# A Hyena block and an adapter on one core: the order of the last stage's products on TensorE, and the rounds in which its steps stand

## What is computed

```python
def _hyena_fwd(x, ...):                       # x is layernorm(x)
    proj = (x @ in_proj_w + in_proj_b).reshape(B, L, C, ORDER + 1)
    v = short_conv(proj[..., 0]) + short_b
    coefs = (gelu(gelu(pos @ fw1 + fb1) @ fw2 + fb2) @ fw3 + fb3).reshape(L, C, ORDER)
    v_fft = rfft(v, n=2 * L, axis=1)
    for i in range(ORDER):
        conv = irfft(v_fft * rfft(coefs[:, :, i], n=2 * L, axis=0)[None], n=2 * L, axis=1)[:, :L, :]
        output = x_branches[i] * conv         # only the last i counts
    return output @ out_w + out_b
x = x + _hyena_fwd(layernorm(x), ...)
x = x + einsum('k,kod,bsd->bso', weights, W[ids], layernorm(x)) + einsum('k,ko->o', weights, b[ids])
```

## Time and profile before

| what | value |
|---|---|
| median of 3 runs (lowest, highest) | 2643.75 us (2641.79, 2646.72) |
| the profiled execution | 2646.0 us, its span 2644.2 us |
| busy over the span: PE, DVE, POOL, ACT | 2415.0, 1463.2, 969.1, 850.0 us |
| granted clock of PE, mean over the span | 0.978 |
| data moved by DMA | 496.59 MB, mean 188 GB/s |

### The profile page before, as it was taken

One profiled execution on the slowest core, in us unless ns is written; L12 is line 12 of the kernel. 1 busy time (PEld: TensorE's weight loads), 2 busy tenths in 40 slices (PEclk: granted clock), 3 DMA queues, 4 the chain that ended last, 5 costly groups with the idle time before them and its releaser, 6 DMA issues. The chain is left out here.

```text
span 2644.2 us, 39549 instructions
## 1 busy us (share of the span) xinstructions
PE 2415.0 (91%) x12804; PEld 1564.5 (59%) x12804; DVE 1463.2 (55%) x2188; ACT 850.0 (32%) x1151; POOL 969.1 (37%) x1189
## 2 busy tenths in 40 slices
PE   6689999999999999699999779989999999999998
PEld 2267777777777776243343356666666666666665
DVE  6634434444443433477776556666666666666665
ACT  3333443343343343244444312222222222222221
POOL 2322222222222222000000056666666666666664
PEclk9789999999999999799999889999999999999999
DMA  5543554544454453899999866555555555555553
GB/s 183 200 124 128 193 165 143 177 145 163 148 173 163 158 164 137 312 343 341 340 344 344 303 190 203 152 155 149 153 151 150 156 149 149 158 150 148 158 151 101
DMA packets 207925, 496.59 MB, mean 188 GB/s; under 512 B 18411, under 2 KB 18732, under 8 KB 190836
## 3 DMA queue, kind: packets, MB, share of 16 engines
q1 hardware_dynamic: 153588, 395.09, 47.2%
q10 hardware_dynamic: 54272, 100.68, 10.2%
HBM read 276.27 MB, written 219.43 MB: 187 GB/s over the span
## 5 line engine op out<-in xcount | busy, mean ns | idle before, releaser
L1034 DVE TENSOR_TENSOR m_m<-m_psA,m_spec 128x1024 f32<-128x1024 f32 x256 | 295.5, 1217 | 149.8 <-PE m_psA L939 128.8
L1194 ACT ACTIVATE b_z<-b_y,b_shift,b_rstd 128x512 f32<-128x512 f32 x128 | 104.2, 814 | 760.0 <-POOL b_shift L1161 760.0
L701 POOL TENSOR_TENSOR vl<-v,vh 128x512 fp32r<-128x512 f32 x128 | 165.6, 1294 | 432.5 <-ACT vh L661 432.5
L956 PE MATMUL m_psW<-m_m,mats 64*64 64x512 f32 x2048 | 249.1, 593 | 0.0
L939 PE MATMUL m_psA<-m_xin,mats 64*64 64x512 f32 x1536 | 203.9, 605 | 42.9 <-DMA m_xin<-spec 32.5
L180 PE MATMUL b_psF<-wfh,b_zh 128*128 128x512 f32 x512 | 215.9, 422 | 1.4 <-DVE b_zl L1297 1.4
L180 PE MATMUL psV<-wvh,nth 128*128 128x512 f32 x512 | 215.7, 421 | 0.0
L180 PE MATMUL b_psO<-woh,b_oh 128*128 128x512 f32 x512 | 212.1, 414 | 0.0
L180 PE MATMUL psG<-wgh,nth 128*128 128x512 f32 x512 | 204.2, 399 | 0.0
L1156 POOL TENSOR_TENSOR b_rstd<-b_mv,b_eps 128x1 f32<-128x1 f32 x128 | 66.9, 523 | 374.6 <-DVE b_mv L1293 374.6
L182 PE MATMUL b_psF<-wfh,b_zl 128*128 128x512 f32 x512 | 203.1, 397 | 0.0
(11 more groups left out here) (122 smaller groups left out, 4602.9 us busy)
## 6 DMA issues: line engine op xcount, KB each, us to landing
m_xin<-spec SPq DMA_DIRECT2D x31, 2304.0 KB, 14.6
spec<-fs1o SPq DMA_DIRECT2D x32, 2048.0 KB, 6.8
spec<-m_wo ACTq DMA_DIRECT2D x64, 1024.0 KB, 10.3
b_fin<-spec SPq DMA_DIRECT2D x128, 512.0 KB, 4.0
xg<-in_L_attn_x_dram SPq DMA_DIRECT2D x64, 512.0 KB, 6.5
gate_d<-gto SPq DMA_DIRECT2D x32, 1024.0 KB, 3.9
b_gin<-gate_d SPq DMA_DIRECT2D x128, 256.0 KB, 3.9
b_xin<-in_L_attn_x_dram SPq DMA_DIRECT2D x256, 128.0 KB, 3.9
```

The lines of the kernel that those rows point to most:

```text
L701: pool.tensor_tensor(vl[:, t % 2], v[:, t % 2], vh[:, t % 2].bitcast(F32), ALU.subtract).then_inc(v_lo, 1)
L956: mm = pe.matmul(psW[pair % 2][half[slot], q, :], ws[slot][half[q]], m[half[q], pair % RM, part, slot, :], start=part == 0, stop=part == 1)
L1034: dve.tensor_tensor(m[:, (k - 2) % RM, part], psA[k % RA][:], spec[:, par, part], ALU.mult).then_inc(m_done, 1)
L1194: act.activation(z[:, t % 2], y[:, t % 2], ACT.Identity, bias=shift[:, t % 2:t % 2 + 1], scale=rstd[:, t % 2:t % 2 + 1]).then_inc(z_done, 1)
```

## The change

The steps' code stays as it is. Only the four lists of the last stage change: their order, and some lags.

```diff
-                pipelined(pool, B, T, [(correct, 0), (scalars, 2), (bias_y, 2)])
+                pipelined(pool, B, T, [(scalars, 3), (bias_y, 3), (correct, 0)])
...
-                pipelined(act, B, T, [(z_high, 3), (o_high, 1), (norm, 2), (store, 6)])
+                pipelined(act, B, T, [(norm, 3), (o_high, 1), (z_high, 4), (store, 6)])
...
-                pipelined(pe, B, T, [(conv, 1), (adapt, 4), (turn_z, 3), (turn_o, 1), (project, 2)])
+                pipelined(pe, B, T, [(conv, 1), (adapt, 5), (turn_o, 1), (turn_z, 4), (project, 2)])
...
-                pipelined(dve, B, T, [(bias_x, 0), (gate, 1), (finish, 4), (z_low, 3), (o_low, 1), (residual, 2)])
+                pipelined(dve, B, T, [(residual, 3), (gate, 1), (finish, 5), (o_low, 1), (z_low, 4), (bias_x, 0)])
```

## The result

The changed kernel takes 2512.0 us (median of four runs, 2507.33 to 2518.87), the kernel before 2645.23 beside it; the ratio of the runs is 0.9499, with a 95% interval of 0.9474 to 0.9524. Timed twice more, it came to 0.9496 (0.9478 to 0.9514) and 0.9499 (0.9485 to 0.9513). The forecast was 2531, with 2520 to 2560 as its range: right in direction and mechanism, 19 us too high, and outside the range. The profiled execution took 2518.87 us with a span of 2516.8; it is the slowest of its four.

What follows compares the result with a forecast made beforehand. The prediction took PE's wait for z in a latency loop as the bound, then PE's own work at 7.75 us a round. Steady rounds -105, start -9, end +2 sum to -112 us, giving 2531; range 2520 to 2560.

Steps and rivals of the forecast that it cites:

- the sum of PE's round: PE's own work in a last-stage round, without waits: 3.68 + 0.32 + 3.43 + 0.32 = 7.75 us, 7.66 to 7.94.
- x: PE's passage from the last matmul of `adapt` to the first transposes: 0.32 us taken, bounds 0.23 and 0.51.
- both sets of transposes and `project`: PE's stretch from the first transposes to the last matmul of `project`: 3.43 us of the round.
- the 2 us for the jumps: Estimated addition to the steady rounds for seven jumps back of the hardware loop, 0.3 us each.
- What bounds the kernel: Last stage before the change: PE's wait for z, 85.3 us in 112 rounds, closes a latency loop of 8.626 us a round.
- PE after the change: PE turns z made the round before, so only its own work remains: 7.75 us a round.
- Start and end: Last stage outside the steady rounds: start gains 9 us (bounds 0 and 11), end loses 2.
- The other engines: DVE, POOL, ACT and SP need no more than PE's 7.75 us; bias_x ends at 7.7, residual is due at 7.85.
- the forecast's own signs of being wrong: PE waiting for o before L1227, residual over 0.15 us after projection's end, or L1273 lasting 1.6 us in most rounds.
- DVE and POOL loop: Rival: the loop residual, scalars, bias_y, correct, bias_x becomes the bound; at 8.0 us a round, 2562 us; chance 0.12.
- The lost interface: Rival: the o product (L1273) loses the interface to bias_y (L1178) each round; round 8.87 us, total 2667; chance 0.05.
- Not shortened: Rival: another wait, such as o_high behind norm, replaces the removed one; round stays 8.6 us, total 2640; chance 0.05.

## Why the prediction was wrong

The step that failed is the sum of PE's round. Its term x, 0.32, measured 0.23; its term for both sets of transposes and `project`, 3.43, measured 3.39; and the 2 us for the jumps measured some 0.3.

**What bounds the kernel: right.** One wait, closed to a loop, held PE up. It is gone, and PE is busy throughout.

**PE after the change: mechanism right, the terms too large.** I took x, the passage from `adapt` to the transposes, as 0.32, from project to conv as the nearest row, and kept 0.23 as the lower end. It is 0.23. The row was near by its types and far by what counts: the size of the stationary operand. Also the part with both sets of transposes and `project` was taken as 3.43 from a round in which the first set had waited; without the wait it is 3.39. That is 0.13 of 7.75 us, 16 us in 123 rounds. The 2 us for the jumps of the loop weren't there either: DVE shows some 0.3 us without work at each of five jumps of the kernel before, but a PE that waits for nobody doesn't inherit it. Steady part: 122.9 gained, 105 forecast, and this difference is nearly all of the error.

**Start and end: near.** 7.0 gained (9 forecast), 2.6 lost (2). In the two later profiles tile 4's conv comes 32.2 and 32.3 us after tile 0's, against 41.3 before: 9 us there. Against its own profiled execution the forecast was 2534 and the time 2518.87, 15 us: 17.9 - 2.0 - 0.6. The other 4 are that I took the profiled execution as 2.25 above the median, as before, and it was 6.9 above it now.

**The other engines: right that they don't bound, one size wrong.** Norm, L1156 and the o product are where they were placed, to 0.2 us. But bias_x takes 1.50, not some 1.1, and ends 7.88 after conv where 7.7 was forecast. So one of the forecast's own signs of being wrong came true: residual started more than 0.15 behind the end of `project` in over half of the rounds. The sign was too strict. Z has a round to spare, and the kernel without bias_x shows that the delay costs nothing.

**The rivals.** *DVE and POOL loop:* not the bound, though residual waits for PE in 13 rounds of 106 only. *The lost interface:* not in the change. But it is what the kernel with the lags alone suffers from, at the price that I gave. I named as what decides whether L1273 comes after 3.25, when bias_y begins, and there it came at 3.74. I had argued that both hang on the same bn_aggr; that a jump of the loop, or the wait for x ahead of gate, can come between bn_aggr and L1273 alone, I hadn't seen. *Not shortened:* no.

**The range.** It held both ends of x, but the low end, 2520, had only x at its lower bound. The 3.39, the two microseconds for the jumps and an ordinary spread of the profiled execution were not in it.

## What to carry to other kernels

In a schedule written out by rounds, look for the product that waits for this round's chain, and give it the round before's: then the chain can take up to about a round more before PE waits for it. (That is the argument of the forecast; no run here makes the chain so long.) Then check what each engine's list begins with and what is queued behind a load, for a delay of 0.3 us on one of two engines that share an interface can cost 1.2. When a passage between two products has no row of its own, choose the nearest by the size of the stationary operand.

## What the runs showed that I had not expected

- From a 512-column matmul of the rounded products to the next one, PE takes 0.22 to 0.24 us at the 2.4 GHz level where both stationary operands have 128 columns, whether the next is rounded or float32; into conv's 64 columns it costs 0.09 more, behind `project` (0.32) as behind a set of transposes (0.53 from the set's start instead of 0.44).
- Two float32 products with 64 columns each, written to the two halves of one tile, ran side by side, 0.007 us apart; with 128 columns each they ran one after the other, and from conv to the second matmul of `adapt` it took 1.95 us instead of 1.35.
- Inside the hardware loop the round that waits for a chain over several engines was longer, the round of a PE that waits for nobody was not: in the kernel before 8.50 outside against 8.5 to 8.9 inside, in the changed one 7.62 in both places.
- The cyclic order of a list being equal, its starting point changes where the jump falls. On DVE the jump shows as 0.32 to 0.59 us without work.
